# One tile-wide sum of squares and 1/std, an earlier first temporal product, and Gelu's table loaded first, in a four-layer conditional residual kernel

## The chip, the cores and the metric

The kernel runs on one core of a Trainium2 chip, in one launch. The metric is the device time of that launch in microseconds, the median of several runs. "PE" is TensorE, "ACT" ScalarE, "DVE" VectorE, "POOL" GpSimd and "SP" SyncE, which only issues DMAs here.

## What is computed

Four residual layers over x of 4 x 1024 x 512, float32:

```python
x = x + concat(gelu(x @ fc1.T + b1) @ fc2.T + b2, gelu(...) @ expert[idx].T + be)   # 512 -> 2048 -> 384 + 128
x = x + x @ W1[subject].T + b[subject]
ctx   = ema(x, tau_ctx)                                       # over the 1024 time steps
gated = x * sigmoid(concat(x, ctx) @ Wg.T + bg)
mod   = 0.5 + sigmoid(gelu(x @ Wn1.T + bn1) @ Wn2.T + bn2)    # 4 rows
temporal = sum_d softmax(blend)[d] * ema(gated * mod[d], tau[d])
gate  = sigmoid(temporal @ Wtemp.T + btemp)
soma  = gelu(x @ Wsoma.T + bsoma)
o     = (soma * gate) @ Wout.T
x = x + (o - mean) / sqrt(var + 1e-5) * gamma + beta
x = x + x @ W3[idx] + b[idx]
```

## The kernel before, in words

The data lie with the 512 features on partitions, in 4 chunks of 128, and time along the free axis. There are 8 tiles of 512 steps, two for each batch entry. Nearly every matrix product is split: both operands are held as a high part (fp32r) and a low rest, and `split_product` (L971 to L974) issues high x high, high x low and low x high into one PSUM bank. ScalarE makes the high parts (copies), VectorE the low ones (`low_part`, L1261). One output chunk of a 512 x 512 layer is therefore 12 matmuls of 128 x 512, a gate product (`gate`, two inputs) 24.

The order of every engine's work is written out by hand, and engines meet at counting semaphores only. `Once` leaves out a wait that an earlier one implies.

First comes the long part, layers 0 and 1: 128 units (8 tiles x 16 chunks of the hidden layer). PE runs fc1(u) and then fc2(u-2). ScalarE applies Gelu in place (L840), then copies the high part (L844), and VectorE makes the low one. Weights are loaded, split and partly parked in DRAM by the way. In the last tile's units the recurrent layer's first tile begins already: n1(0), mo(0), gate(0,0) to gate(0,3). mod_of(0) (L866) stands at the end of ScalarE's unit 9 of that tile.

Then come the rounds r = 1 to 7, one for each tile. In a steady round PE issues: n1(r), rb(r-2), gate(r,0), mo(r), te(r-1,0..3), gate(r,1), gate(r,2), l3(r-2,0..3), gate(r,3), ou(r-1,0..3), so(r,0), so(r,1), ss(r-1), so_pair(r). Round 1 is joined to the end of the long part and has gate(1,0), l1(7,3), gate(1,1), te(0,..), gate(1,2), gate(1,3), ou(0,..). Here n1 and mo give the modulation (h1_of and mod_of on ScalarE; POOL adds 2, stores the 4 rows and loads them back to all partitions as mod_t). `gate` gives Wg's product. VectorE scans it (scan_g), ScalarE applies tanh, and traces_a to traces_d (VectorE) make the four moving averages of a chunk and their sum `temporal`. `temporal_hi` (ScalarE) and `temporal_low` (VectorE) split it for te. te_tanh, spikes, spikes_hi and spikes_low lead on to ou. `o_of` copies and squares ou's result, and sum_squares adds the four squares into sumsq.

The normalisation before the change: ss multiplies sumsq, four blocks of 128 steps as the weights, by one column of ones (L1146). The sums over the 512 features lie then as 128 x 4. rows_std takes the square root (L811), rows_rstd the reciprocal (L1477), and four tensor_scalar (L1483) write them on the diagonals of `diag`. rb multiplies four of these by ones (L1157), which spreads 1/std over all partitions in PSUM bank 6. z_of multiplies by it and gamma (L1490), x3_of adds beta and the residual (L1496). x3_hi_of and x3_low split the result for l3, whose output y_of reads.

The tail, after round 7, is rb(6), te(7,..), l3(6,0), ou(7,..), l3(6,1), ss(7), l3(6,2), rb(7), l3(6,3), and at last l3(7) chunk by chunk. On VectorE rows_rstd(r-1) stands between traces_c(r,3) and traces_d(r,3), and temporal_low(r) behind them.

Bank 0 serves te(0), ou(0) and the row sums; bank m serves te, ou and l1 of the last tile.

Of the kernel before, what the change touches and what calls it, by code (L numbers as in the profile page):

```python
# [8 lines left out]
ALU = mybir.AluOpType  # L9
# [3 lines left out]
P = 128  # L13
# [28 lines left out]
def build(nc, x, tok16, tok8, small, fc1_w, fc2_w, exp_w, exp_b, l1_w, l1_b, wg, wn1, wsoma, wtemp, wout,  # L42
# [13 lines left out]
    with ctx:  # L56
# [12 lines left out]
        def sem(name):  # L69
# [60 lines left out]
        std = const("std", TOK // P)  # L130
        rstd = const("rstd", TOK // P)
# [3 lines left out]
        diag = const("diag", TOK)  # L135
# [49 lines left out]
                ("L1", "N1", "SO", "MO", "WG", "TE", "OU", "SS", "RB", "L3")}  # L185
# [26 lines left out]
        s_diag = sem("s_diag")  # L212
# [116 lines left out]
        SS_BANK, RB_BANK = bank[0], bank[6]  # L329
# [341 lines left out]
        def _(eng):  # L671
# [135 lines left out]
            def rows_std(i):  # L807
                on.wait_ge(s_pe["SS"], i + 1)
                if i:
                    on.wait_ge(s_rstd, i)  # L810
                eng.activation(std[:, :], SS_BANK[:, 0:TOK // P], ACT.Sqrt, bias=eps_sb[:, 0:1],  # L811
                               scale=1.0 / DIM).then_inc(s_std, 1)
# [16 lines left out]

            fc1_hi(0)  # L830
# [5 lines left out]
            for u in range(UNITS):  # L836
                t, j = divmod(u, HC)
                ps = fc1_bank(u)
                on.wait_ge(s_fc1, u + 1)
# [25 lines left out]
                if t == LAST and j == 9:  # L865
                    mod_of(0)  # L866
# [43 lines left out]
            for m in range(SH):  # L910
                temporal_hi(1, m)

            for r in range(2, NT):
                h1_of(r)
                temporal_hi(r - 1, 3)
# [24 lines left out]
                for m in range(SH):  # L940
                    temporal_hi(r, m)

            temporal_hi(LAST, 3)
# [9 lines left out]
            on.wait_ge(s_rstd, LAST)  # L953
            eng.activation(std[:, 0:1], eps_sb[:, 0:1], ACT.Sqrt).then_inc(s_chain, 1)
# [13 lines left out]
        def _(eng):  # L968
# [75 lines left out]
            def gate(i, m):  # L1044
# [27 lines left out]
                for c in range(KC):  # L1072
                    x2 = slot(i, c)
                    for k, before in ((2 * c, 0), (2 * c + 1, 1)):
# [4 lines left out]
                                           c == KC - 1 and before == 1)  # L1079
                mm.then_inc(s_pe["WG"], 1)  # L1080

            def te(i, m):
                if m == 0:
                    if i:
                        on.wait_ge(s_std, i)
                    else:
                        on.wait_ge(s_x2, KC * NT)
                elif m >= 2:
# [52 lines left out]
            def ss(i):  # L1141
# [3 lines left out]
                for q in range(TOK // P):  # L1145
                    mm = eng.matmul(SS_BANK[:, q:q + 1], sumsq[:, q * P:(q + 1) * P], ones[:, 0:1],  # L1146
                                    start=True, stop=True)
                mm.then_inc(s_pe["SS"], 1)

            def rb(i):  # L1150
                if i < LAST:
                    on.wait_ge(s_gated, KC * (i + 1) + 3)
# [595 lines left out]
```

## Time and profile before

| | us |
|---|---|
| median of 3 runs | 1387.55 (1387.07 to 1387.76) |
| the profiled execution | 1386.63 |
| its span, first to last instruction | 1384.6 |
| PE busy | 1366.0 (99%) |
| DVE busy | 761.2 (55%) |
| ACT busy | 479.9 (35%) |
| POOL busy | 136.2 (10%) |

The span is what the profile covers; the rest of the execution's time lies around it. A row of the time line has its start, its busy time, engine, line, operation, output<-input and count; a bracket tells how long the engine had been idle and whose end released it. Matmuls overlap: one of 128 x 512 is busy for 0.39 us and the next starts 0.23 us after it, so distances are read from start to start. A float32 matmul shows as two records.

### The profile page before, as it was taken

To read this page: it belongs to the slowest core of one execution; us is meant where nothing else is said; L and a number is where in the kernel's file an instruction comes from. 1 tells how busy PE (TensorE), PEld (TensorE's weight loads), DVE (VectorE), ACT (ScalarE), POOL (GpSimd) and SP (SyncE) were. 2 spreads that over 40 slices of the span, in tenths; PEclk is the share of its full clock that TensorE was granted. 3 is DMA by queue.
4 is the path that set the end of the run, shared out by engine and by line. 5 is a ranking of instruction groups with operands and counts; after the bars stand their busy time and mean duration, and the time that the engine had idled before them with its cause. 6 is when DMAs were issued, how large, how long until landed. Compare 5 with 4: busy or idle time off the path is not lost.

```text
span 1384.6 us, 15423 instructions
## 1 busy us (share of the span) xinstructions
PE 1366.0 (99%) x6024; PEld 1119.0 (81%) x6024; DVE 761.2 (55%) x1067; ACT 479.9 (35%) x799; POOL 136.2 (10%) x170
## 2 busy tenths in 40 slices
PE   9999999999999999999999999899999999999998
PEld 7888888888888888888887888678787878787877
DVE  3344242232342332333221793999797979797993
ACT  5443342332342332333221221334334343424253
POOL 5000100000100000000000220013101210032000
PEclk9999999999999999999999999999999999999999
DMA  5423522502532413423133934711232123211201
GB/s 132 137 69 122 137 99 107 152 31 84 154 124 80 129 69 111 127 97 97 41 107 114 219 124 154 177 66 61 92 122 93 61 92 122 92 62 61 92 0 61
DMA packets 68376, 140.91 MB, mean 102 GB/s; under 512 B 7328, under 2 KB 19616, under 8 KB 64336
## 3 DMA queue, kind: packets, MB, share of 16 engines
q1 hardware_dynamic: 61360, 116.71, 26.9%
q0 software_dynamic: 6944, 23.23, 5.6%
q8 instruction: 47, 0.77, 0.2%
q14 instruction: 25, 0.20, 0.1%
HBM read 86.85 MB, written 53.05 MB: 101 GB/s over the span
## 4 chain that ended last, share of the span: by engine, by line
PE 90%; DVE 7%; DMA 1%; issue 1%; ACT 1%; POOL 0%; SPq 0%; DVEq 0%; POOLq 0%; ACTq 0%
PE bank L972 30%; PE bank L973 29%; PE bank L974 29%; DVE drive L1417 2%; DVE drive L1402 1%; DVE temporal L1427 1%; DVE temporal L1417 1%; PE bank L1039 1%; PE bank L1157 0%; DVE spikes_lo L1261 0%; DMA x_slot<-x2hl_dram 0%; DVE bank L1378 0%; DMA mod_t<-mod_dram 0%; PE bank L1146 0%; DMA x_raw<-in_x 0%
## 5 line engine op out<-in xcount | busy, mean ns | idle before, releaser
L1261 DVE TENSOR_TENSOR h_hl<-bank,h_hl 128x512 fp32r<-128x512 f32 x128 | 88.7, 693 | 472.8 <-ACT h_hl L844 472.8
L972 PE MATMUL bank<-x_hl,wa 128*128 128x512 f32 x512 | 199.7, 390 | 1.4 <-DVE h_hl L1261 0.8
L974 PE MATMUL bank<-x_hl,wa 128*128 128x512 f32 x512 | 199.2, 389 | 0.0
L973 PE MATMUL bank<-x_hl,wa 128*128 128x512 f32 x512 | 199.2, 389 | 0.0
L972 PE MATMUL bank<-h_hl,wa 128*128 128x512 f32 x512 | 199.2, 389 | 0.0
L973 PE MATMUL bank<-h_hl,wa 128*128 128x512 f32 x512 | 199.2, 389 | 0.0
L974 PE MATMUL bank<-h_hl,wa 128*128 128x512 f32 x512 | 199.2, 389 | 0.0
L840 ACT ACTIVATE bank<-bank,small_sb 128x512 f32<-128x512 f32 x128 | 84.2, 658 | 216.7 <-PE bank L974 216.5
L844 ACT ACTIVATE h_hl<-bank 128x512 fp32r<-128x512 f32 x128 | 76.7, 599 | 231.5 <-PE bank L974 231.1
L972 PEld LDWEIGHTS bank<-x_hl,wa 128*128 128x128 f32 x512 | 96.1, 188 | 23.7 <-issue 2.7
L974 PEld LDWEIGHTS bank<-x_hl,wa 128*128 128x128 f32 x512 | 96.1, 188 | 20.1
L973 PEld LDWEIGHTS bank<-h_hl,wa 128*128 128x128 f32 x512 | 96.2, 188 | 20.0
L974 PEld LDWEIGHTS bank<-h_hl,wa 128*128 128x128 f32 x512 | 96.1, 188 | 19.9
L972 PEld LDWEIGHTS bank<-h_hl,wa 128*128 128x128 f32 x512 | 96.0, 188 | 19.9
L973 PEld LDWEIGHTS bank<-x_hl,wa 128*128 128x128 f32 x512 | 96.0, 188 | 19.7
L1402 DVE SCALAR_TENSOR_TENSOR drive<-gated,small_sb,mod_t 128x512 f32<-128x512 f32 x128 | 92.1, 740 | 35.9 <-DMA mod_t<-mod_dram 34.2
L972 PE MATMUL bank<-x_slot,wg_hl 128*128 128x512 f32 x256 | 101.2, 395 | 1.3 <-ACT mod_row L740 1.3
L973 PE MATMUL bank<-x_slot,wg_hl 128*128 128x512 f32 x256 | 99.8, 390 | 0.0
L974 PE MATMUL bank<-x_slot,wg_hl 128*128 128x512 f32 x256 | 99.4, 388 | 0.0
L628 POOL DMA_DIRECT2D x2hl_dram<-x_hl x28 | 21.1, 770 | 606.4 <-DVE x_hl L1261 606.4
L1427 DVE TENSOR_TENSOR temporal<-drive,temporal 128x512 f32<-128x512 f32 x96 | 66.1, 688 | 1.2
L1261 DVE TENSOR_TENSOR x_hl<-x_raw,x_hl 128x512 fp32r<-128x512 f32 x96 | 61.7, 685 | 1.3 <-ACT x_hl L718 1.3
(154 smaller groups left out, 2323.8 us busy)
## 6 DMA issues: line engine op xcount, KB each, us to landing
x_slot<-x2hl_dram SPq DMA_DIRECT2D x32, 513.0 KB, 4.8
x2hl_dram<-x_hl POOLq DMA_DIRECT2D x28, 512.0 KB, 9.3
stage<-in_l_w SPq DMA_DIRECT2D x32, 256.0 KB, 3.1
x_dram<-x_raw SPq DMA_DIRECT2D x8, 1024.0 KB, 5.4
xt<-x_dram SPq DMA_DIRECT2D x8, 1024.0 KB, 5.7
mod_t<-mod_dram POOLq DMA_DIRECT2D x8, 1024.0 KB, 4.9
l3w_hl<-l3w_dram SPq DMA_DIRECT2D x16, 512.0 KB, 6.8
x_raw<-in_x SPq DMA_DIRECT2D x7, 1024.0 KB, 9.0
```

The source lines that it names most:

```text
L628: eng.dma_start(x2hl_dram[t, c, :, :, 1:1 + TOK], x_hl[t % 2][:, :, c, :].bitcast(F32)).then_inc(s_hlst[c], 16)
L840: eng.activation(ps[:, :], ps[:, :], ACT.Gelu, bias=fc1_b_sb[:, j:j + 1]).then_inc(s_gelu, 1)
L844: eng.activation(h_hl[u % 2][:, 0, :], ps[:, :], ACT.Copy).then_inc(s_hhi, 1)
L972: eng.matmul(ps, w_hi, x_hi, start=first, stop=False)
L973: eng.matmul(ps, w_hi, x_lo, start=False, stop=False)
L974: return eng.matmul(ps, w_lo, x_hi, start=False, stop=final)
L1039: eng.matmul(mo_bank(i)[0:TAUS, :], wn2_sb, h1[:, :], start=True, stop=True).then_inc(s_pe["MO"], 1)
L1261: return eng.tensor_tensor(lo, raw, hi.bitcast(F32), ALU.subtract)
L1402: eng.scalar_tensor_tensor(drive[d % 2][:, :], gated[:, :], blend_sb[:, TAUS * c + d:TAUS * c + d + 1], mod_t[:, d, :], ALU.mult, ALU.mult ...
L1417: eng.tensor_tensor_scan(traced, alpha[:, 1 + d:2 + d].to_broadcast([P, TOK]), drive[d % 2][:, :], start, ALU.mult, ALU.add).then_inc(s_tr ...
L1427: eng.tensor_tensor(temporal[:, c, :], drive[d % 2][:, :], temporal[:, c, :], ALU.add).then_inc(s_add, 1)
```

## The change

1. A one-column Gelu is ScalarE's first instruction. 2. mod_of(0) moves ahead of the wait for fc1 in its unit. 3. In round 1 gate(1,1) moves behind te(0,..), and VectorE's order there follows (x2_lo and spikes earlier, scan_g(1,1) later); te(0,m) waits for the last tile's x2 chunk by chunk. 4. ss becomes one product of 128 x 128 ones with sumsq, which leaves the sum on every partition; the square root and the reciprocal are taken over 128 x 512 in SBUF, z_of reads that, and diag and rb are gone. 5. mo(r) goes inside gate(r,0), behind its first 6 matmuls, and temporal_hi(r-1,2) behind h1_of(r). 6. rows_rstd(r-1) moves between the two halves of temporal_low(r), in the last round behind both.

```diff
@@ -127,12 +127,10 @@
         eps_sb = const("eps_sb", 1)
         g_last = const("g_last", KC)
         trace_last = const("trace_last", KC * TAUS)
-        std = const("std", TOK // P)
-        rstd = const("rstd", TOK // P)
         zeros = const("zeros", 2)
         ones = const("ones", P)
         ident = const("ident", P)
-        diag = const("diag", TOK)
+        rstd = const("rstd", TOK)
         stage_hi = nc.alloc_sbuf_tensor_at("stage_hi", [P, TOK], F32R, offset=constants_at[0] - 4 * TOK)
 
         bank = [ctx.enter_context(nc.psum_tensor(f"bank{i}", [P, TOK], F32)) for i in range(8)]
@@ -182,7 +180,7 @@
         s_exp = sem("s_exp")
         s_id = sem("s_id")
         s_pe = {k: sem("s_pe_" + k) for k in
-                ("L1", "N1", "SO", "MO", "WG", "TE", "OU", "SS", "RB", "L3")}
+                ("L1", "N1", "SO", "MO", "WG", "TE", "OU", "SS", "L3")}
         s_x2free = sem("s_x2free")
         s_g = sem("s_g")
         s_glast = sem("s_glast")
@@ -209,7 +207,6 @@
         s_ssq = sem("s_ssq")
         s_std = sem("s_std")
         s_rstd = sem("s_rstd")
-        s_diag = sem("s_diag")
         s_z = sem("s_z")
         s_x3 = sem("s_x3")
         s_x3hi = sem("s_x3hi")
@@ -326,7 +323,7 @@
         def l3_bank(i, m):
             return bank[((7, 4, 7, 4) if i < LAST else (1, 2, 3, 5))[m]]
 
-        SS_BANK, RB_BANK = bank[0], bank[6]
+        SS_BANK = bank[0]
 
 
         def x2_at(i, c):
@@ -807,8 +804,11 @@
             def rows_std(i):
                 on.wait_ge(s_pe["SS"], i + 1)
                 if i:
-                    on.wait_ge(s_rstd, i)
-                eng.activation(std[:, :], SS_BANK[:, 0:TOK // P], ACT.Sqrt, bias=eps_sb[:, 0:1],
+                    on.wait_ge(s_z, KC * i)
+                else:
+                    on.wait_ge(s_psthi, 16 * len(PARKED))
+                    on.wait_ge(s_stlo, STAGED)
+                eng.activation(rstd[:, :], SS_BANK[:, :], ACT.Sqrt, bias=eps_sb[:, 0:1],
                                scale=1.0 / DIM).then_inc(s_std, 1)
 
             def x3_hi_of(i, m):
@@ -827,6 +827,9 @@
                 eng.activation(to, l3_bank(i, m)[:, :], ACT.Identity, bias=l3_b_sb[:, b * KC + m:b * KC + m + 1]
                                ).then_inc(s_y, 1)
 
+
+            on.wait_ge(s_cst, 1)
+            eng.activation(g_last[:, 0:1], eps_sb[:, 0:1], ACT.Gelu)
             fc1_hi(0)
             for c in range(KC):
                 x_hi(0, c)
@@ -836,6 +839,8 @@
             for u in range(UNITS):
                 t, j = divmod(u, HC)
                 ps = fc1_bank(u)
+                if t == LAST and j == 9:
+                    mod_of(0)
                 on.wait_ge(s_fc1, u + 1)
                 eng.activation(ps[:, :], ps[:, :], ACT.Gelu, bias=fc1_b_sb[:, j:j + 1]).then_inc(s_gelu, 1)
                 on.wait_ge(s_gelu, u + 1)
@@ -862,8 +867,6 @@
                         l1_hi(b, j - L1_UNIT - KC)
                 if t == LAST and j == 8:
                     h1_of(0)
-                if t == LAST and j == 9:
-                    mod_of(0)
                 if t and x2_unit(t - 1) <= j < x2_unit(t - 1) + 2:
                     x2_hi(t - 1, 2 * (j - x2_unit(t - 1)))
                     x2_hi(t - 1, 2 * (j - x2_unit(t - 1)) + 1)
@@ -907,11 +910,12 @@
             rows_std(0)
             soma_of(1, 2)
             soma_of(1, 3)
-            for m in range(SH):
-                temporal_hi(1, m)
+            temporal_hi(1, 0)
+            temporal_hi(1, 1)
 
             for r in range(2, NT):
                 h1_of(r)
+                temporal_hi(r - 1, 2)
                 temporal_hi(r - 1, 3)
                 mod_of(r)
                 wg_tanh(r, 0)
@@ -937,9 +941,10 @@
                 rows_std(r - 1)
                 soma_of(r, 2)
                 soma_of(r, 3)
-                for m in range(SH):
-                    temporal_hi(r, m)
-
+                temporal_hi(r, 0)
+                temporal_hi(r, 1)
+
+            temporal_hi(LAST, 2)
             temporal_hi(LAST, 3)
             te_tanh(LAST, 0)
             for m in range(KC):
@@ -950,8 +955,8 @@
             for m in range(KC):
                 spikes_hi(LAST, m)
 
-            on.wait_ge(s_rstd, LAST)
-            eng.activation(std[:, 0:1], eps_sb[:, 0:1], ACT.Sqrt).then_inc(s_chain, 1)
+            on.wait_ge(s_z, KC * LAST)
+            eng.activation(rstd[:, 0:1], eps_sb[:, 0:1], ACT.Sqrt).then_inc(s_chain, 1)
             y_of(LAST - 1, 0)
             for m in range(KC):
                 o_of(LAST, m)
@@ -1077,15 +1082,16 @@
                                            x2[:, 0, at:at + TOK],
                                            x2[:, 1, at:at + TOK], c == 0 and not before,
                                            c == KC - 1 and before == 1)
+                    if m == 0 and c == 0 and i > 1:
+                        mo(i)
                 mm.then_inc(s_pe["WG"], 1)
 
             def te(i, m):
-                if m == 0:
-                    if i:
-                        on.wait_ge(s_std, i)
-                    else:
-                        on.wait_ge(s_x2, KC * NT)
-                elif m >= 2:
+                if i == 0:
+                    on.wait_ge(s_x2, KC * LAST + m + 1)
+                elif m == 0:
+                    on.wait_ge(s_std, i)
+                if m >= 2:
                     on.wait_ge(s_soma, KC * i + m + 1)
                 on.wait_ge(s_wtemp, 16 * KC)
                 for c in range(KC):
@@ -1142,21 +1148,8 @@
                 on.wait_ge(s_cst, 1)
                 on.wait_ge(s_sq, KC * i + 1)
                 on.wait_ge(s_ssq, SH * (i + 1))
-                for q in range(TOK // P):
-                    mm = eng.matmul(SS_BANK[:, q:q + 1], sumsq[:, q * P:(q + 1) * P], ones[:, 0:1],
-                                    start=True, stop=True)
-                mm.then_inc(s_pe["SS"], 1)
-
-            def rb(i):
-                if i < LAST:
-                    on.wait_ge(s_gated, KC * (i + 1) + 3)
-                else:
-                    on.wait_ge(s_z, KC * LAST)
-                for q in range(TOK // P):
-                    on.wait_ge(s_diag, (TOK // P) * i + q + 1)
-                    mm = eng.matmul(RB_BANK[:, q * P:(q + 1) * P], ones[:, :], diag[:, q * P:(q + 1) * P],
-                                    start=True, stop=True)
-                mm.then_inc(s_pe["RB"], 1)
+
+                eng.matmul(SS_BANK[:, :], ones[:, :], sumsq[:, :], start=True, stop=True).then_inc(s_pe["SS"], 1)
 
             def l3_part(i, m, c):
                 return split_product(l3_bank(i, m)[:, :], l3w_hl[c][:, 0, m * P:(m + 1) * P],
@@ -1212,17 +1205,13 @@
             mo(1)
             gate(1, 0)
             l1(LAST, 3)
-            gate(1, 1)
             for r in range(1, NT):
                 if r > 1:
                     n1(r)
-                    rb(r - 2)
                     gate(r, 0)
-                    mo(r)
                 for m in range(KC):
                     te(r - 1, m)
-                if r > 1:
-                    gate(r, 1)
+                gate(r, 1)
                 gate(r, 2)
                 if r > 1:
                     for m in range(KC):
@@ -1234,7 +1223,6 @@
                 so(r, 1)
                 ss(r - 1)
                 so_pair(r)
-            rb(LAST - 1)
             for m in range(KC):
                 te(LAST, m)
             l3(LAST - 1, 0)
@@ -1243,7 +1231,6 @@
             l3(LAST - 1, 1)
             ss(LAST)
             l3(LAST - 1, 2)
-            rb(LAST)
             l3(LAST - 1, 3)
             on.wait_ge(s_soma, KC * LAST + 2)
             for c in range(KC):
@@ -1447,11 +1434,10 @@
                 trace_of(i, c, 3)
                 add_of(i, c, 3)
 
-            def temporal_low(i):
-                for p in (0, 2):
-                    on.wait_ge(s_temphi, KC * i + p + 2)
-                    low_part(temporal_lo[:, p:p + 2, :], temporal[:, p:p + 2, :], ts_hi[:, p:p + 2, :]
-                             ).then_inc(s_templo, 2)
+            def temporal_low(i, p):
+                on.wait_ge(s_temphi, KC * i + p + 2)
+                low_part(temporal_lo[:, p:p + 2, :], temporal[:, p:p + 2, :], ts_hi[:, p:p + 2, :]
+                         ).then_inc(s_templo, 2)
 
             def spikes(i, m):
                 on.wait_ge(s_gate, KC * i + m + 1)
@@ -1474,20 +1460,13 @@
 
             def rows_rstd(i):
                 on.wait_ge(s_std, i + 1)
-                eng.reciprocal(rstd[:, :], std[:, :]).then_inc(s_rstd, 1)
+                eng.reciprocal(rstd[:, :], rstd[:, :]).then_inc(s_rstd, 1)
+
+            def z_of(i, m):
                 on.wait_ge(s_rstd, i + 1)
-                on.wait_ge(s_id, 3)
-                if i:
-                    on.wait_ge(s_pe["RB"], i)
-                for q in range(TOK // P):
-                    eng.tensor_scalar(diag[:, q * P:(q + 1) * P], ident[:, :], rstd[:, q:q + 1], None, ALU.mult
-                                      ).then_inc(s_diag, 1)
-
-            def z_of(i, m):
-                on.wait_ge(s_pe["RB"], i + 1)
                 on.wait_ge(s_o, KC * i + m + 1)
                 o = o_of_tile(i)[:, m, :]
-                eng.scalar_tensor_tensor(o, o, gamma_sb[:, m:m + 1], RB_BANK[:, :], ALU.mult, ALU.mult
+                eng.scalar_tensor_tensor(o, o, gamma_sb[:, m:m + 1], rstd[:, :], ALU.mult, ALU.mult
                                          ).then_inc(s_z, 1)
 
             def x3_of(i, m):
@@ -1594,21 +1573,23 @@
             traces_d(0, 3)
             x2_of(LAST, 0)
             x2_of(LAST, 1)
-            temporal_low(0)
+            temporal_low(0, 0)
+            temporal_low(0, 2)
             x2_of(LAST, 2)
             scan_g(1, 0)
             x2_of(LAST, 3)
             traces_a(1, 0)
-            traces_b(1, 0)
             for c in range(KC):
                 x2_lo(LAST, c)
-            scan_g(1, 1)
+            for m in range(SH):
+                spikes(0, m)
+            traces_b(1, 0)
+            spikes(0, 3)
             traces_c(1, 0)
-            traces_d(1, 0)
-            for m in range(KC):
-                spikes(0, m)
             spikes_low(0, 0, 2)
             spikes_low(0, 2, 2)
+            traces_d(1, 0)
+            scan_g(1, 1)
             traces_a(1, 1)
             traces_b(1, 1)
             scan_g(1, 2)
@@ -1622,10 +1603,11 @@
             traces_d(1, 2)
             traces_a(1, 3)
             traces_b(1, 3)
-            rows_rstd(0)
             traces_c(1, 3)
             traces_d(1, 3)
-            temporal_low(1)
+            temporal_low(1, 0)
+            rows_rstd(0)
+            temporal_low(1, 2)
             for r in range(2, NT):
                 norm_of(r - 2)
                 scan_g(r, 0)
@@ -1656,10 +1638,13 @@
                 traces_a(r, 3)
                 traces_b(r, 3)
                 traces_c(r, 3)
-                rows_rstd(r - 1)
                 traces_d(r, 3)
-                temporal_low(r)
-
+                temporal_low(r, 0)
+                if r < LAST:
+                    rows_rstd(r - 1)
+                temporal_low(r, 2)
+
+            rows_rstd(LAST - 1)
             norm_of(LAST - 1)
             spikes(LAST, 0)
             x3_low(LAST - 1, 0, 2)
```

## Rows read from the trace of the kernel before

**Rows 1.** The page: busy us (share of the span), instructions of PE.

```profile
PE 1366.0 (99%) x6024; PEld 1119.0 (81%) x6024; DVE 761.2 (55%) x1067; ACT 479.9 (35%) x799; POOL 136.2 (10%) x170
```

**Rows 2.** Time line of ACT and PE at the start of the kernel.

```profile
3.66 0.63 ACT L676 ACTIVATE wa<-stage_early 128x512 fp32r<-128x512 f32 x1 [1.50 <-DMA stage_early<-in_fc_w]
...
10.19 1.28 ACT L840 ACT_TABLE_LOAD   x1 [0.58 <-PE bank L974]
...
12.44 0.39 PE L974 MATMUL bank<-x_hl,wa 128*128 128x512 f32 x1
13.65 0.47 PE L972 MATMUL bank<-x_hl,wa 128*128 128x512 f32 x1 [0.82 <-DVE h_hl L1261]
```

**Rows 3.** Time line of ACT and PE at mod_of(0) and gate(0,0).

```profile
744.11 0.66 ACT L840 ACTIVATE bank<-bank,small_sb 128x512 f32<-128x512 f32 x1 [5.38 <-PE bank L974]
...
748.10 0.50 PE L972 MATMUL bank<-x_slot,wg_hl 128*128 128x512 f32 x1 [1.31 <-ACT mod_row L740]
```

**Rows 4.** Time line of PE in round 1: ou(0) and ss(0).

```profile
871.38 0.47 PE L972 MATMUL bank<-ts_hi,wout_hl 128*128 128x512 f32 x1 [4.46 <-DVE spikes_lo L1261]
...
891.58 1.04 PE L1146 MATMUL bank<-ones,sumsq 128*128 128x1 f32 x8 [2.00 <-DVE sumsq L1473]
```

**Rows 5.** Time line of PE in the tail.

```profile
1333.97 0.47 PE L972 MATMUL bank<-ts_hi,wtemp_hl 128*128 128x512 f32 x1 [2.52 <-DVE temporal_lo L1261]
...
1348.34 0.47 PE L972 MATMUL bank<-ts_hi,wout_hl 128*128 128x512 f32 x1 [0.52 <-DVE spikes_lo L1261]
...
1362.06 0.95 PE L1146 MATMUL bank<-ones,sumsq 128*128 128x1 f32 x8
1362.87 0.49 PE L972 MATMUL bank<-x_hi,l3w_hl 128*128 128x512 f32 x1
...
1365.73 1.05 PE L1157 MATMUL bank<-diag,ones 128*128 128x128 f32 x8
1366.54 0.48 PE L972 MATMUL bank<-x_hi,l3w_hl 128*128 128x512 f32 x1
...
1369.80 0.50 PE L972 MATMUL bank<-ts_hi,l3w_hl 128*128 128x512 f32 x1 [0.26 <-DVE x_lo L1261]
```

**Rows 6.** Windows: length, busy of PE, PEld, DVE, ACT, POOL; PEclk; DMA.

```profile
871.00:876.00 5.00, 4.62 (x13) 3.70 (x14) 4.96 (x7) 0.31 (x1) 0.00 (x0) 0.66 1.04 152
889.00:896.00 7.00, 5.00 (x20) 3.90 (x19) 6.79 (x9) 3.31 (x5) 0.00 (x0) 0.76 0.00 0
1330.00:1336.00 6.00, 3.39 (x19) 2.71 (x18) 5.97 (x10) 3.14 (x6) 0.00 (x0) 1.00 0.01 3
```

**Rows 7.** Time line of DVE in round 1.

```profile
856.05 1.28 DVE L1417 TENSOR_TENSOR_SCAN temporal<-alpha,trace_last,drive 128x512 f32<-128x512 f32 x1 [13.65 <-PE bank L974]
...
872.28 0.69 DVE L1386 SCALAR_TENSOR_TENSOR gated<-bank,xt 128x512 f32<-128x512 f32 x1
...
907.91 2.35 DVE L1261 TENSOR_TENSOR temporal_lo<-temporal,ts_hi 128x1024 fp32r<-128x1024 f32 x2
```

**Rows 8.** Time line of PE: mo(7) and the start of te(6,0).

```profile
1267.99 1.02 PE L1039 MATMUL bank<-h,small_sb 128*4 128x512 f32 x2
1268.94 0.50 PE L972 MATMUL bank<-ts_hi,wtemp_hl 128*128 128x512 f32 x1
```

**Rows 9.** Groups of DVE by line: busy us, mean ns of one, idle before.

```profile
L1477 DVE RECIPROCAL rstd<-std 128x4 f32<-128x4 f32 x8 | 1.4, 173 | 2.5 <-ACT std L811 2.5
...
L1366 DVE RECIPROCAL alpha<-alpha 128x5 f32<-128x5 f32 x1 | 0.2, 192 | 0.0
...
L1368 DVE TENSOR_SCALAR alpha_minus<-alpha 128x1 f32<-128x1 f32 x1 | 0.2, 154 | 0.0
```

**Rows 10.** Time line of DVE in the last round.

```profile
1321.58 0.68 DVE L1386 SCALAR_TENSOR_TENSOR gated<-bank,xt 128x512 f32<-128x512 f32 x1
...
1329.89 0.88 DVE L1483 TENSOR_SCALAR diag<-ident,rstd 128x128 f32<-128x128 f32 x4
...
1334.88 2.71 DVE L1490 SCALAR_TENSOR_TENSOR o_sb<-o_sb,small_sb,bank 128x512 f32<-128x512 f32 x4
```

## The prediction

> **What bounds the kernel now.** I read the page first: PE is busy for 99% of the span, so a removed TensorE instruction is worth its full spacing wherever the engine does not wait, and the other gains can only be its waits [rows 1]. Then I followed PE in order of time and looked at each bracket (idle time and what ended it). Five places stand out. At the start, the third fc1 unit begins 1.21 us after the product ahead of it, because ScalarE loaded Gelu's table for 1.28 us only once the first unit was there [rows 2]. At 748 us the first gate product waits 1.31 us for mod_of(0) [rows 3]. In round 1 the output product waits 4.46 us for spikes_lo and the sum over rows 2.00 us for sumsq [rows 4]. Before te(LAST) it waits 2.52 us for temporal_lo [rows 5]. Products otherwise follow each other every 0.2275 us (60 of them, 13.72 us less fills, from the start of ou(LAST) to the sum over rows at 1362.06 [rows 5]); so 12, 24 and 48 products are 2.7, 5.45 and 10.9 us.
>
> The clock view shows a second price of the round 1 waits: the granted clock averages 0.66 over 5 us after the first, which is 3.4 us at 1.2 instead of 2.4 GHz, and 0.76 over 7 us around the second, again 3.4 us. Work done at half speed for 3.4 us loses 1.7 us each. Around the 2.52 us wait at 1331 the clock stayed at the upper level [rows 6].
>
> **The change part by part**, in the time of the profiled execution.
>
> (a) Table. The new Gelu of one column waits only for eps_sb and brings the load ahead of the first copy, which anyway starts only at 3.66 us, waiting for a DMA [rows 2]. Then the first real Gelu starts 1.28 us earlier, and fc1(2) would be ready before PE is (13.65 - 1.28 = 12.37, PE at 12.67). PE gets 13.65 - 12.67 = **1.0 us**. The next limit is PE itself.
>
> (b) mod_of(0) ahead of the Gelu: MO's product stands a whole unit ahead of this gate in PE's order, and ScalarE is idle for 5.38 us until 744.11, so the tanh is done before the Gelu and gate(0,0) no longer waits: **1.3 us** [rows 3]. The modulation rows leave earlier on POOL's queue, where nothing is pushed back by it.
>
> (c) te(0) ahead of gate(1,1). PE was ready for ou(0) at 871.38 - 4.46 = 866.9; before that stood te(0) (10.9) and three gate products (16.35), so te(0) can start at 839.6 and ends at 850.5, 5.45 earlier than the 855.97 at which VectorE's trace scan was released. In the 13.65 us VectorE was idle there [rows 7] now fit the four x2_lo and three spikes, seven operations of 0.6 to 0.7 us (4.4 in all). From the scan at 856.05 to gated(1,1) at 872.28 are 16.2 us of work; the 4.4 leave it and a tanh round trip of 0.9 comes in. Gated(1,1) is then at 850.5 + 16.2 - 4.4 + 0.9 = 863.2, nearly **9 us earlier**. spikes_lo is done near 859.5, PE needs it at 866.9: the 4.46 us go, and the low clock after it, 1.7: **6.2 us**. The sum of squares, ready at 891.5, is ready at 882.6; PE, ready at 889.6 before, comes at 889.6 - 6.2 = 883.4. The 2.00 us go too, with their 1.7 of low clock: **3.7 us**, on a margin of only 0.8.
>
> (d) RB. Each broadcast takes 0.81 us from its start to the next product's (1365.73 to 1366.54). Six stand ahead of te(LAST-1): **4.9 us**; the other two are in the tail below. In exchange the sum over rows, 0.81 before (1362.06 to 1362.87), becomes one 512-column float32 product by 128 weights [rows 5]. The nearest row is MO, also float32 with 512 columns: 0.95 from start to start [rows 8]. Bounds: 0.8 (nothing) and 1.4. I take 0.95, 0.15 more, for six **-0.9 us**. MO itself only moves inside gate(r,0). It comes 6 products after n1, at +1.36; the Gelu it needs ends at about 0.16 + 0.1 + 0.69 = 0.95 (the N1 result's end, the start, the activation). So nothing waits, and the modulation starts 4 us earlier.
>
> (e) Reciprocal. VectorE now takes it over 128x512, once a tile, in place of 0.17 and the four diag products (0.88) [rows 9, 10]. No row shows this size. Small ones do: 128x4 takes 173 ns and 128x5 192, while a plain operation on one column takes 154 [rows 9]. That makes 6.3 ns per element (19/3) or 9.5 (38/4), and from the two reciprocals alone 19. If all of it were fixed cost, 512 elements would take about 0.6, as other VectorE operations do. I take 8 ns, between the first two: **R = 4.2 us**. Ends kept for the range: 0.6 and 9.9. The square root goes from 0.26 to 0.66 us as any 128x512 ScalarE operation with a bias [rows 3]; it runs in the table pair that is there now.
> The Trainium skill, in "VectorE: DVE Perf Modes", section "First, the fixed hardware budget", says that Reciprocal is an iterative divide with a repeat count of 8; with that page's 0.96 GHz it is 8.3 ns per element, an estimate of 4.4 us, and the sum would be 0.6 worse than with my value. It speaks against this part of the change.
>
> (f) Where R lands. In most rounds temporal_low(r,0), R, temporal_low(r,2) stand between the last trace and te(r), and PE first runs n1 and the gate. In the last round now the trace chain starts from sumsq: gated at 1321.58, te(LAST) at 1333.97, 12.4 us, less 1.05 for the old reciprocal and diag = 11.35 [rows 5, 10]. With T the start of te(r-1) (1268.94 before [rows 8]), ou ends at T + 49.1 (48 x 4 + 24 products), the last square at 50.5, gated at 51.15, so te's first half is ready at T + 62.5, its second with R at 67.9; PE asks at 70.9 and 72.2. Rounds 3 to 6 have 4 us to spare. **Round 2** has not: the traces of tile 1 end at 907.91 - 8.9 - 1.05 = 897.95 [rows 7], the first low half is ready at 899.3, R follows, the second half at 904.7. PE, from 883.4 on, does 0.95 + 60 products + 0.95 and asks for the first at 898.9, for the second at 900.7. It waits 0.4 + 4.0 = **-4.4 us**, and since this is nearly the wait that took the clock down before [rows 4, 6], **-1.7** more.
>
> (g) Tail. te(LAST) started at T + 65.03, now at T + 62.5. The reciprocal of tile LAST-1 now stands ahead of its norm: z began 0.91 after te's start [rows 5, 10], now 5.1. Four z, four x3 and a spike, nine operations of 0.66, follow, so x3_low begins at 11.0. l3(LAST-1,0), due at 10.9, waits 1.3; the last three spikes come at 13.3 to 15.1, spikes_lo after them, ou at +16.5 instead of 14.37. That is T + 79.0 against 79.4. From ou, the last tile's sum of squares ends at +14.7, square root +15.5, R +19.75, then z, x3, copy and low part (3.0) +22.8, where l3(LAST) began at +21.46 before (1369.80 - 1348.34 [rows 5]). T + 101.8 against 100.86: **-0.9 us**.
>
> **Sum**: 1.0 + 1.3 + 6.2 + 3.7 + 4.9 - 0.9 = 16.2; less 4.4, 1.7 and 0.9 = 9.2 us. The profiled execution took 1386.63 us (span 1384.6), 0.9 under the median 1387.55. 1386.6 - 9.2 = 1377.4, and with the 0.9 near the median 1378.3; I say **1378.0 us**.
>
> **Rivals.**
> - Reciprocal at the speed of other operations (R = 0.6). For it: the operation count is the same as a copy's. Against: it is 19 ns dearer than a plain operation at 128x4. The round 2 wait shrinks to 0.9 and keeps its clock, ou starts at T + 62.5 + 14.4 = 76.9, and l3(LAST) 20.4 later, when PE is free: 97.3, a gain of 3.6. 16.2 - 0.9 + 3.6 = 18.9: 1367.7, against the median 1368.5. Chance 0.15.
> - Slower than before: R is 9.9 us (19 ns per element, the difference of the two reciprocals). Round 2 loses 10.1 + 1.7, the tail 0.9 + 2 x 5.7 = 12.3, and rounds 3 to 6 and the one between are past their slack (62.5 + 9.9 + 1.2 = 73.6 against 72.2), 1.4 five times. 16.2 - 31.1 = -15: about 1402. It decides from R = 4.2 + 9.2/3 = 7.3 us (14 ns per element). For it: only one pair of rows; against: the other two slopes. Chance 0.06, and 0.06 that R lies near 7 and all cancels (1384.8 to 1390.3).
> - The round 1 gain is not had in full: the sum of squares misses its margin of 0.8 us and the clock falls there again, or MO waits for h1 in each of six rounds (0.4 us to spare). Some 3 us dearer: 1381. Chance 0.11.
> - That the table is loaded again: copies and tanhs follow Gelu without a load now, so it would need another set. Its price is (a), 1 us, inside the range.
> My forecast has 0.62. What remains open in it is 1.7 us of clock either way (round 2, or the 2.6 us wait before l3(LAST)).
>
> **Numbers.** About 0.2%, 2.8 us, is what a measurement can tell from no change. Faster 0.88, same 0.06, slower 0.06. The range is 1368 (fast reciprocal, just held) to 1385 (R near 6.5 with both clock losses).
>
> **What would show it.** No PE wait at 13, 748, ou(0) and ss(0), and clock 1.00 there; the sum over rows as two float32 passes with 0.95 to the next product; no broadcast; RECIPROCAL 128x512 near 4.2 us; PE waits 4 us for temporal_lo at te(1) and has a low clock behind it, 1 to 2 us at l3(LAST-1,0) and ou(LAST), 2 to 3 at l3(LAST); none in rounds 3 to 6. The prediction is wrong if the reciprocal is not near 4.2 us, or if te(0)'s move leaves VectorE where it was.

## The result and the profile after

The changed kernel takes **1374.59 us** in the median (4 runs, 1371.03 to 1374.97) beside 1387.65 us of the kernel before on the same chip (4 runs, 1387.07 to 1388.50). The ratio is 0.990, 95% interval 0.9882 to 0.9917: 13.1 us faster. 1378.0 was forecast. Sign and range held, and the gain came out larger. The profiled execution took 1374.9 us (span 1373.2) against 1386.63 before (span 1384.6), 11.7 less where the sum said 9.2.

The page of the changed kernel, engines first, then the group of VectorE's modulation multiplies and the group of its reciprocals (busy us, mean ns, idle time before and what ended it):

```profile
PE 1359.0 (99%) x5912; PEld 1109.7 (81%) x5912; DVE 781.5 (57%) x1035; ACT 480.9 (35%) x799; POOL 134.4 (10%) x170
...
L1389 DVE SCALAR_TENSOR_TENSOR drive<-gated,small_sb,mod_t 128x512 f32<-128x512 f32 x128 | 92.0, 739 | 2.6 <-DMA mod_t<-mod_dram 0.6
...
L1463 DVE RECIPROCAL rstd<-rstd 128x512 f32<-128x512 f32 x8 | 26.8, 3345 | 3.0 <-ACT rstd L811 3.0
```

PE is still busy for 99% [rows 1]. The reciprocal over 512 columns takes 3345 ns, against 173 for the old one [rows 9]. The waits of the changed kernel's PE, grouped (us in total, times, longest):

```profile
PE bank L977 <- DVE temporal_lo L1248: 6.3, 3, 3.2
PE bank L977 <- DVE x_lo L1248: 1.6, 1, 1.6
PE bank L1179 <- DVE eps_sb L1491: 1.2, 1, 1.2
PE bank L977 <- DVE spikes_lo L1248: 0.5, 1, 0.5
```

mod_row and sumsq are gone from that list, and spikes_lo has only the 0.5 of the tail left. temporal_lo, 2.52 in the tail before [rows 5], now has 6.3 in three places. In order of time on the changed kernel's PE (start, us, instruction, idle before):

```profile
746.20 0.39 PE L977 MATMUL bank<-x_slot,wg_hl 128*128 128x512 f32 x1
...
864.74 0.40 PE L977 MATMUL bank<-ts_hi,wout_hl 128*128 128x512 f32 x1
...
881.07 1.02 PE L1152 MATMUL bank<-sumsq,ones 128*128 128x512 f32 x2
...
897.40 0.47 PE L977 MATMUL bank<-ts_hi,wtemp_hl 128*128 128x512 f32 x1 [0.45 <-DVE temporal_lo L1248]
...
898.63 0.39 PE L979 MATMUL bank<-ts_hi,wtemp_hl 128*128 128x512 f32 x1
901.64 0.79 PE L977 MATMUL bank<-ts_hi,wtemp_hl 128*128 128x512 f32 x1 [2.62 <-DVE temporal_lo L1248]
902.24 0.63 PE L978 MATMUL bank<-temporal_lo,wtemp_hl 128*128 128x512 f32 x1
...
914.23 0.39 PE L977 MATMUL bank<-x_slot,wg_hl 128*128 128x512 f32 x1
...
1240.49 1.02 PE L1152 MATMUL bank<-sumsq,ones 128*128 128x512 f32 x2
1240.94 0.80 PE L977 MATMUL bank<-x_slot,wsoma_hl 128*128 128x512 f32 x1
1241.58 0.40 PE L978 MATMUL bank<-x_slot,wsoma_hl 128*128 128x512 f32 x1
...
1256.30 0.40 PE L977 MATMUL bank<-ts_hi,wtemp_hl 128*128 128x512 f32 x1
...
1310.87 1.02 PE L1152 MATMUL bank<-sumsq,ones 128*128 128x512 f32 x2
...
1320.61 0.52 PE L977 MATMUL bank<-ts_hi,wtemp_hl 128*128 128x512 f32 x1 [3.23 <-DVE temporal_lo L1248]
...
1336.58 0.47 PE L977 MATMUL bank<-ts_hi,wout_hl 128*128 128x512 f32 x1 [0.52 <-DVE spikes_lo L1248]
...
1358.45 0.50 PE L977 MATMUL bank<-ts_hi,l3w_hl 128*128 128x512 f32 x1 [1.64 <-DVE x_lo L1248]
```

The rows answer to [rows 3] (746.20), [rows 4] (864.74 and 881.07) and [rows 5] (from 1320.61 on). The first three start without a bracket: the old waits are gone. The new cost stands at te(1). From 897.40 to the next gate product at 914.23 are 16.83 us, where the kernel before needed 11.05, from these rows of its PE:

```profile
910.71 0.50 PE L972 MATMUL bank<-ts_hi,wtemp_hl 128*128 128x512 f32 x1
...
921.76 0.39 PE L972 MATMUL bank<-x_slot,wg_hl 128*128 128x512 f32 x1
```

Of the 5.8 more, 2.8 are the wait (898.63 plus one spacing of 0.23 to 901.64), and 3.0 come from the slow products behind it, whose starts are 0.43 apart instead of 0.23. The windows of the changed kernel show the clock (length, busy of PE, PEld, DVE, ACT, POOL; then PEclk, the granted clock as a share of 2.4 GHz, and DMA):

```profile
866.00:871.00 5.00, 5.00 (x24) 4.14 (x23) 5.00 (x7) 2.38 (x4) 0.00 (x0) 1.00 0.89 304
902.00:908.00 6.00, 6.00 (x15) 4.64 (x15) 6.00 (x9) 0.00 (x0) 0.00 (x0) 0.51 0.43 175
1321.00:1325.00 4.00, 4.00 (x12) 3.14 (x11) 3.96 (x3) 0.00 (x0) 0.00 (x0) 0.59 0.00 0
```

After ou(0) began the clock is at the full 2.4 GHz, where it had been 0.66 [rows 6]. Behind the wait of te(1) it is 1.2 GHz for nearly 6 us, and behind that of te(LAST) again for 3.3 of 4.

Where did the profiled gain come from? The lead of each step's start over the same step before is (gate(r,m) and n1(r) of round r, the others of their tile): gate(0,0) 1.9 us, ou(0) 6.6, ss(0) 10.5, n1(2) 12.2, gate(2,0) 13.9, te(1) 13.3, gate(2,1) 7.5, te(LAST-1) 12.6, te(LAST) 13.4, ou(LAST) 11.8, l3(LAST) 11.35, end 11.4. It climbs through round 1, falls by 5.8 inside te(1), and is won again at a steady 1.0 us a round.

### The profile page after: what moved, and what is told of

It is laid out like the page before. It is cut to its first block, busy times and chain, and to the rows that moved or that the text cites. A ratio compares the mean times of both kernels' runs of the same rounds, so it can differ in the third digit from the quotient of the medians.

```text
span 1373.2 us, 15160 instructions
## 1 busy us (share of the span) xinstructions
PE 1359.0 (99%) x5912; PEld 1109.7 (81%) x5912; DVE 781.5 (57%) x1035; ACT 480.9 (35%) x799; POOL 134.4 (10%) x170
## 4 chain that ended last, share of the span: by engine, by line
PE 93%; DVE 4%; DMA 1%; ACT 1%; issue 0%; SPq 0%; DVEq 0%
PE bank L977 31%; PE bank L978 31%; PE bank L979 31%; DVE drive L1404 1%; DMA x_slot<-x2hl_dram 1%; DVE drive L1389 1%; DVE rstd L1463 0%; PE bank L1044 0%; DVE temporal L1414 0%; PE bank L1152 0%; DMA x_raw<-in_x 0%; DVE temporal L1404 0%; DVE bank L1365 0%; DVE temporal_lo L1248 0%; ACT temporal L827 0%
```

## The experiments

They were timed in three sets (e1 to e4; e5 to e8; e9 and e10). The kernel before took 1390.43, 1389.69 and 1388.77 us in them, so only the ratios compare across sets.

**The changed kernel again** (e8), as the control of the second set.

> The changed kernel itself, on the same chip as the others of this set, to compare them with it. All theories: 12 to 15 us below the kernel before. By my theory of the low clock its runs spread over 3 to 4 us, one or two losses of 1.7 us or more after the waits in te(1) and before te(7) being there or not, while those waits themselves (2.6 and 3.2 us) stay.

Measured: 1375.76 us, ratio 0.9896 (0.9879 to 0.9912), -13.9 us. The two long waits are the same, 2.62 at te(1) and 3.23 at te(LAST). The four runs spread over 4.0 us, as expected. Between its first weight and 60 us PE waits 4.5 us in all, where the first trace has 0.4. The longest is 1.82; the Gelu ahead of it stood behind a weight copy of ScalarE that had itself waited 2.98 us for its load:

```profile
43.34 0.47 PE L977 MATMUL bank<-x_hl,wa 128*128 128x512 f32 x1 [1.82 <-DVE h_hl L1248]
```

**The normalisation alone** (e1): parts (d) to (g), with te(0), the gate order, mod_of(0) and the table as before. (MO stays where it was too.)

```diff
-                for q in range(TOK // P):
-                    mm = eng.matmul(SS_BANK[:, q:q + 1], sumsq[:, q * P:(q + 1) * P], ones[:, 0:1],
+                eng.matmul(SS_BANK[:, :], ones[:, :], sumsq[:, :], start=True, stop=True)
...
-            rb(LAST - 1)
...
+                eng.reciprocal(rstd[:, :], rstd[:, :]).then_inc(s_rstd, 1)
```

> The changed normalisation alone on the kernel before: no early table, mod_of(0), te(0), VectorE's round 1 and mo(r) where they were. My theory: the broadcast's products are worth 1.0 us a round (five rounds 5.1) and 1.6 in round 2, but the reciprocal of 3.35 us between the two halves of temporal_low then makes PE wait about 2.2 us in te(1), with 1.7 to 3 us of low clock behind it, and the tail gives 1 us back: 1 to 4.5 us faster than before, that is 1383 to 1386.5. The waits of 4.5 us before ou(0) and 2.0 before ss(0) stay. Rival: the normalisation carries most of the gain, as its 8 broadcasts and 8 sums are the only TensorE work that changes: 8 us or more faster.

Measured: 1384.42 us, ratio 0.9961 (0.9948 to 0.9975), **-6.0 us**, more than the 1 to 4.5 that I expected. The profiled execution doesn't show as much: its span ends 2.9 us under the first trace of the kernel before (1381.7 against 1384.6), after 0.47 lost at the start. The old waits at ou(0) (4.46) and ss(0) (2.29, where it had been 2.00) stay, and te(LAST) waits 3.24. te(1) waits only 1.95, with the clock at 1.00 behind it. The reason lies one step earlier, and e2 below shows it: behind ss(0) the clock is low here, so that PE comes to te(1) later after ss(0).

**te(0)'s move alone** (e10): part (c) on the kernel before, old normalisation.

```diff
             l1(LAST, 3)
-            gate(1, 1)
...
-                if r > 1:
-                    gate(r, 1)
+                gate(r, 1)
```

(and with it VectorE's order of round 1, and te(0,m) waiting for x2 chunk by chunk.)

> The kernel before with te(0) ahead of gate(1,1) and VectorE's new order of round 1, nothing else: diag, RB and the reciprocal over 128x4 stay. My theory: the waits before ou(0) and ss(0) and the low clock behind them go (10 us), RB of tile 0 waits about 1 us longer for diag, and te(1) has no wait, since that one is the long reciprocal's: 9 us faster than before. Rival: VectorE is short in round 2 without the reciprocal as well: te(1) waits 2 us or more and the gain is 4 to 6.

Measured: 1379.59 us, ratio 0.9937 (0.9923 to 0.9951), **-9.2 us**. Its PE in time order:

```profile
866.71 0.40 PE L972 MATMUL bank<-ts_hi,wout_hl 128*128 128x512 f32 x1
...
883.04 0.95 PE L1145 MATMUL bank<-ones,sumsq 128*128 128x1 f32 x8
...
894.29 1.13 PE L1156 MATMUL bank<-diag,ones 128*128 128x128 f32 x8 [1.86 <-DVE diag L1480]
```

Both waits and both stretches of low clock are gone. te(1) has no wait either: that one belongs to the long reciprocal. The broadcast instead waits 1.86 for diag, which the full change doesn't have, since it has no broadcast.

**te(0)'s move undone** (e2), all else as changed: the same lines in the other direction.

> The changed kernel with te(0) behind gate(1,1) again, and VectorE's order of round 1 with it. My theory: this move is worth 8.6 us (4.5 + 2.0 of waits and 1.6 to 1.7 of low clock after each, less fills) and the wait in te(1) stays about as long, since VectorE and PE are later by the same: 1383. Rival: most of it is only moved to te(1), so that without it te(1) has no wait: the wait of 2.8 us and 3.1 of low clock there go, and the time is 1377 to 1378.

Measured: 1385.18 us, ratio 0.9962 (0.9949 to 0.9976), -5.25 us, so some 9 us (0.9962 against the control's 0.9896) are lost without the move. The waits at ou(0) (4.46) and ss(0) (1.57) are back, and te(1) keeps its 0.45 and 2.62, as expected:

```profile
906.59 0.47 PE L977 MATMUL bank<-ts_hi,wtemp_hl 128*128 128x512 f32 x1 [0.45 <-DVE temporal_lo L1250]
...
910.84 0.50 PE L977 MATMUL bank<-ts_hi,wtemp_hl 128*128 128x512 f32 x1 [2.62 <-DVE temporal_lo L1250]
```

The windows behind ss(0), of e1 and then of this run:

```profile
892.00:900.00 8.00, 7.96 (x26) 5.81 (x27) 7.93 (x10) 5.58 (x7) 0.00 (x0) 0.80 0.29 87
```

```profile
890.00:898.00 8.00, 8.00 (x34) 6.26 (x35) 7.93 (x10) 6.96 (x10) 0.00 (x0) 1.00 0.42 133
```

Both runs lack the move, and VectorE takes 17.75 us from the start of the sum of squares to te(1)'s first low half in both (889.62 to 907.37, 887.48 to 905.23), as in the changed kernel (878.28 to 896.03). PE takes 17.32 us from ss(0) to te(1) in e1 without a wait, and 16.70 here with one of 0.45. So the shorter wait of e1 goes with the low clock (and the longer sum product, 2.05 us) ahead of it, not with the missing move.

**Parts (a) and (b) undone** (e9).

```diff
-            on.wait_ge(s_cst, 1)
-            eng.activation(g_last[:, 0:1], eps_sb[:, 0:1], ACT.Gelu)
...
-                if t == LAST and j == 9:
-                    mod_of(0)
```

(mod_of(0) stands behind the unit's Gelu again.)

> The changed kernel without the early Gelu and with mod_of(0) behind the Gelu of its unit again. My theory: both gains are PE's waits and nothing later makes them up: 0.8 us before the third fc1 unit and 1.3 us at gate(0,0) are back, with their fills 2.4 us, 1377 to 1378 where the changed kernel is at 1375. Rival: the first weights' arrival paces the start, so the table's part is lost in it: only 1.5 us slower.

Measured: 1376.24 us, ratio 0.9909 (0.9895 to 0.9922). The control's ratio was 0.9896, so 1.8 us with overlapping intervals: the timing alone doesn't show it, and it can't tell my 2.4 from the rival's 1.5. In the trace the waits of 0.79 (h_hl, third unit) and 1.31 (mod_row, gate(0,0)) are there, which the changed kernel doesn't have. Whether the first of them is worth its microsecond is another question. Eight traces have the early Gelu (the first, e2 to e8). Seven of them show PE waits of 0.2 to 1.8 us somewhere between 18 and 56 us, and none of the four without it does (before, e1, e9, e10). gate(0,0) starts at 746.2 to 750.0 with it, 747.7 in the mean, and at 748.0 to 748.6 without it, 748.3 in the mean, of which about 1.4 is mod_row's wait and its slow start. Up to that wait the kernels with the early Gelu are thus 0.8 us later in the mean, not 1.0 earlier: (b)'s gain is seen there, (a)'s is not, and the rival stands, that the loads pace the start. Why the later waits come is open; the sets ran on different chips.

**MO back behind the gate** (e7).

```diff
-                    if m == 0 and c == 0 and i > 1:
-                        mo(i)
...
                     gate(r, 0)
+                    mo(r)
```

> The changed kernel with mo(r) behind gate(r,0) again and temporal_hi(r-1,2) ahead of h1_of(r). My theory: VectorE waits some 5 us more for mod_t in each round, but the chain starts anew from ou's squares, so te(2) to te(7) do not notice: within 0.5 us of the changed kernel, and te(1) has the same waits. Rival: the earlier modulation is what keeps VectorE ahead of PE, so that without it te(r) waits in every round: 5 us or more slower than the changed kernel.

Measured: 1375.57 us, 0.2 from the control in the same set. VectorE's wait for mod_t is 18.6 us with MO back, 34.2 in the kernel before and 0.6 with the change. None of it can be seen at PE: 18 us of idle time taken off an engine, worth nothing that can be measured.

**The reciprocal behind both halves of temporal_low** (e3). My theory was that the wait in te(1) is the reciprocal's place in VectorE's order.

```diff
             temporal_low(1, 0)
-            rows_rstd(0)
             temporal_low(1, 2)
+            rows_rstd(0)
```

(and in each later round but the last, where it stood there already.)

> The changed kernel with the reciprocal behind both halves of temporal_low in every round. My theory: the wait of 2.6 us in the midst of te(1,0) is the reciprocal's alone, and the low clock of 6 us behind it (3.1 us lost) is the wait's: both go, 5.9 us faster than the changed kernel, 1368.7. Rival: the low clock comes whatever the wait (the 0.45 us before te(1) is enough): only 2.8 us faster, 1371.8.

Measured: 1370.85 us, ratio 0.9864 (0.9849 to 0.9879), **-19.6 us**. The ratio lies 4.4 to 5.0 us under the changed kernel's (0.9896 and 0.9900), less than the 5.9 expected and more than the rival's 2.8. The waits in te(1) are gone, and the clock there is 1.00. A smaller one takes their place in l3(0,2): l3(0) now needs 12.2 us (919.52 to 931.68) for 10.9 to 11.0, since ScalarE's y for this bank stands behind a gate's copy and tanh, which waited 4.1 us for VectorE's scan. te(LAST) still waits 3.23, ou(LAST) 1.06 instead of 0.52. From the trace of this version, VectorE, then PE:

```profile
896.20 2.35 DVE L1248 TENSOR_TENSOR temporal_lo<-temporal,ts_hi 128x1024 fp32r<-128x1024 f32 x2
898.47 3.35 DVE L1463 RECIPROCAL rstd<-rstd 128x512 f32<-128x512 f32 x1
```

```profile
928.82 0.50 PE L977 MATMUL bank<-x_hi,l3w_hl 128*128 128x512 f32 x1 [0.97 <-ACT y_sb L827]
```

**temporal_hi(LAST) ahead of the last two somas** (e4). The trace of the changed kernel shows why te(LAST) waits longer than worked out. ScalarE, then VectorE:

```profile
1316.74 1.37 ACT L777 ACTIVATE soma<-bank,small_sb 128x512 f32<-128x512 f32 x2 [1.68 <-PE bank L979]
1318.00 2.17 ACT L756 ACTIVATE ts_hi<-temporal 128x512 fp32r<-128x512 f32 x4
```

```profile
1319.24 2.36 DVE L1248 TENSOR_TENSOR temporal_lo<-temporal,ts_hi 128x1024 fp32r<-128x1024 f32 x2 [1.65 <-ACT ts_hi L756]
```

The copies stand behind two Gelus that wait for PE. The edit, for the last tile alone:

```diff
                 rows_std(r - 1)
+                if r == LAST:
+                    for m in range(KC):
+                        temporal_hi(LAST, m)
                 soma_of(r, 2)
                 soma_of(r, 3)
```

(and out of their old places.)

> The changed kernel with ScalarE's four temporal_hi of the last tile ahead of its soma_of(7,2) and (7,3). My theory: te(7) waits 3.2 us for ScalarE, which takes the two Gelus first, not for VectorE's traces: te(7) starts 1.7 us earlier and all behind it, and with the shorter wait the low clock behind it (1.6 us) may go too: 1371.3 to 1372.9. Rival: VectorE's traces are the limit, as in my prediction: no change, 1374.6.

Measured: 1372.90 us, ratio 0.9878 (0.9863 to 0.9894), -17.5 us, some 2.5 to 3 under the changed kernel by the ratios. te(1) keeps its 2.62 and its low clock. VectorE and PE now:

```profile
1317.49 2.35 DVE L1250 TENSOR_TENSOR temporal_lo<-temporal,ts_hi 128x1024 fp32r<-128x1024 f32 x2
```

```profile
1318.85 0.47 PE L979 MATMUL bank<-ts_hi,wtemp_hl 128*128 128x512 f32 x1 [1.50 <-DVE temporal_lo L1250]
```

The low parts follow the traces without a gap, and the wait is 1.50. From ss(LAST-1) to te(LAST) are 8.0 us instead of 9.74. 0.4 and 0.6 of it come back as waits at l3(LAST-1,0) and ou(LAST).

**Both orders together** (e5).

> The reciprocal behind both halves of temporal_low, and the last tile's temporal_hi ahead of two Gelus, together. My theory: the two are 420 us apart and add up: 2.8 us for te(1) and 1.7 for te(7), against the changed kernel, less 0.9 lost at l3(0,2) and 1 in the tail's norm, plus the low clock that went after both waits (1.7 to 3 us each, where it is there): 3 to 7 us faster than the changed kernel. Rival: the tail's norm (waits before l3(6,0), ou(7) and l3(7)) takes all of the second gain: no faster than the reciprocal's move alone, 3 to 4 us.

Measured: **1369.98 us** (1369.38 to 1370.29), ratio 0.9856 (0.9840 to 0.9873), 5.8 us under the control. It beats both kernels. The clock windows of this version, at te(1) and te(LAST):

```profile
900.00:908.00 8.00, 8.00 (x36) 6.35 (x35) 7.96 (x8) 0.45 (x1) 3.43 (x3) 1.00 0.20 81
1316.00:1324.00 8.00, 7.62 (x34) 6.32 (x35) 7.96 (x9) 2.99 (x4) 0.00 (x0) 1.00 0.00 0
```

**A shorter reciprocal** (e6): it covers 128 of the 512 time steps, and 1/std of the other 384 is left out.

```diff
-                eng.reciprocal(rstd[:, :], rstd[:, :]).then_inc(s_rstd, 1)
+                eng.reciprocal(rstd[:, 0:P], rstd[:, 0:P]).then_inc(s_rstd, 1)
```

> The changed kernel with the reciprocal over 128 of the 512 steps only (384 steps of 1/std are left out, so this part of the output is scaled wrongly): some 0.9 us for 3.35. My theory, that the reciprocal costs about three times its length (once in te(1), twice in the tail, less what other waits hide): the wait of 2.6 us in te(1) falls to 0.2 and its low clock goes, the wait of 1.6 before l3(7) goes, the one before ou(7) and the 3.2 before te(7) stay: 4 to 7 us faster than the changed kernel. Rival: the reciprocal is hidden nearly everywhere and the waits have other causes: under 1.5 us.

Measured: 1369.37 us, ratio 0.9859 (0.9842 to 0.9875), 6.4 under the control. The second wait in te(1) is down to 0.23 at full clock and the one at l3(LAST) is gone; the first in te(1) (0.40) and te(LAST)'s 3.23 stay.

So the reciprocal's length costs the changed kernel about 6 us. The orders of e3 and e4 together give 5.8 without shortening it, but not all of it in the same places: in e5 the 1.64 before l3(LAST) stays, and 1.7 come from te(LAST), where the reciprocal had no part.

## Why the prediction was right, and where its sizes were off

- **(a) Table**: the wait is gone, and in the first trace its time is gained: a few products into the third unit 0.9 for 1.0 (the first product began 0.46 later in this execution, so the net lead stood at 0.43). Over all traces the gain is not shown. The working ended with "the next limit is PE itself", and in seven of the eight traces with the early Gelu PE waits again before 60 us (e9).
- **(b) mod_of(0)**: right. gate(0,0) adds 1.5 for 1.3. The wait is 1.30 or 1.31 in the four kernels that lack this part and absent in the others.
- **(c) te(0)**: right in mechanism and size. Gated(1,1) is at 861.40 (863.2 forecast), both waits and both low clocks are gone, 10.3 us from gate(0,0) to n1(2) for 9.9. The rival of an incomplete gain fell, and e10 shows 9.2 by itself.
- **(d) Broadcast and sum over rows**: this is the term that was mis-sized. Six broadcasts at 0.81 less six sums at 0.15 were 4.0 us; the traces give 6.8. The first part is a wait that I had not listed, 0.52 for diag at the broadcast of round 2 (below), which with its slow start makes 1.7 of gate(2,0)'s lead. The rest is five later rounds at 1.0 instead of 0.66. The distance to the first product behind the broadcast, 0.81 [rows 5], is not all: the second starts 1.13 us behind the broadcast's start, which is 0.90 more than a plain spacing. And the sum over rows is not 0.15 dearer. From its start to the second product behind it are 1.09 us (1240.49 to 1241.58), against 1.13 for the four small products (1323.68 to 1324.81) and 1.30 for MO (1267.99 to 1269.29). MO was the wrong neighbour. A round without a wait, from sum to sum, is 71.47 us before (1252.21 to 1323.68) and 70.38 after (1240.49 to 1310.87): 1.09, of which some 0.14 are in neither term; what they are stays open.

PE of the kernel before, at the broadcast of round 2 and at two sums over rows:

```profile
903.19 1.13 PE L1157 MATMUL bank<-diag,ones 128*128 128x128 f32 x8 [0.52 <-DVE diag L1483]
...
1252.21 0.94 PE L1146 MATMUL bank<-ones,sumsq 128*128 128x1 f32 x8
...
1323.68 0.95 PE L1146 MATMUL bank<-ones,sumsq 128*128 128x1 f32 x8
```

- **(e) Reciprocal**: 3.35 us for 4.2, 6.5 ns per element. That is near the lowest of my three slopes, from the plain operation to the reciprocal of four columns (19/3 = 6.3), and not the value of 8 that I took; from 128x4 to 128x512 it is 6.2 (3172 ns over 508 columns). By the Trainium skill, "VectorE: DVE Perf Modes", section "First, the fixed hardware budget", I had an estimate of 4.4, and this case's measurement is a quarter below it. The rivals of 0.6 and 9.9 fell.
- **(f) Round 2**: right place, and a right sum by luck, from two wrong parts. Waits 0.45 and 2.62 for 0.4 and 4.0 (the shorter reciprocal and the earlier second half), but the clock stayed low for some 6 us, not 3.4: 3.0 lost for 1.7. That is 6.2 in all for 6.1. In four other executions the clock was low for 3.3 us only, and in one it stayed high (last section). Rounds 3 to 6 have no wait on it. e3 and e6 show that the reciprocal's place and length set it.
- **(g) Tail**: -0.9 forecast, -1.3 measured. With T the start of te(LAST-1), the chain to te(LAST) was worked out on VectorE alone: T + 62.5. It came at T + 64.3 (1320.61 - 1256.30), since ScalarE takes two somas ahead of the copies. e4, with that order changed, brings te(LAST) forward by 1.74, to T + 62.6. Its 1.6 us of low clock were not forecast. The later steps made up for most of that, ou at te + 15.97 (16.5) and l3(LAST) at ou + 21.87 (22.8), because the reciprocal is shorter. The wait of 1.3 forecast at l3(LAST-1,0) did not come, since the slow products of te(LAST) hid it; at full clock it is 0.43 (e4).
- **The sum**: 9.2 forecast against 11.4 at the end of the span. (d) makes up 2.8 of the difference, the rest cancels to -0.6. From profile to median another 1.4 come in: the profiled execution of before lay 1.0 below its median, that of after 0.3 above.
- **MO**: nothing, and e7 finds nothing.

So the forecast named what happens and where. Its closeness, 1378.0 for 1374.59, is in part luck: in (f) two errors cancel, and only because the profiled execution had the longest low clock at te(1) of all.

Do the parts add up? The move alone brings 9.2, and everything without the move 5.25 (e2): 14.4, near the 13.1 and 13.9 measured together. The normalisation alone brought 6.0, and with it, the move and (a) and (b) the count would be some 17. The excess thus lies between e1 and e2, which both lack the move. In the traces e1 waits less in te(1) (1.95 at full clock; e2 has 0.45 and 2.62 with 0.79 over 8 us), after losing time to a low clock behind ss(0) that e2 doesn't have. What the clock did in each execution differs, so the 6.0 can't be split further.

## What to carry to other kernels

When work is taken off one engine and given to another as one long operation, its length matters less than what stands behind it in that engine's order: here 3.35 us in front of half an operand made te(1) 3 to 6 us longer, by what the clock did behind the wait, and behind it l3(0) 1.2 us longer. Work out the time of a step that joins two engines on both queues, since a copy behind someone else's wait is late by that wait. And measure a small group of instructions by the distance between plain products on either side of it, not to the first start behind it.

## What the runs showed that was not expected

- **The same wait, another clock.** A wait of 2.62 to 2.64 us in te(1) was followed by a granted clock of 0.79 to 0.81 over 8 us in e2, e4, e8 and e9 (1.2 GHz for some 3.3 us), by nearly 6 us of 1.2 GHz in the changed kernel's first trace, and by none in e7 (1.00), whose kernel differs in MO's place. The wait of 3.2 us before te(LAST) gave 0.63 over 8 us in e8, 0.65 in e7, 0.82 in e6 and 1.00 in e3. What decides stays open: no run varied it on purpose. It may be part of the spread: the changed kernel's four runs in e8's set lie between 1374.3 and 1378.3, those of e5 in the same set, whose clock is 1.0 in all four, within 0.9 us. The windows behind the wait in e8 and in e7:

```profile
905.47:913.47 8.00, 8.00 (x28) 6.52 (x29) 7.07 (x10) 1.56 (x4) 0.23 (x1) 0.79 0.36 131
```

```profile
902.78:910.78 8.00, 8.00 (x35) 6.61 (x36) 7.07 (x10) 1.56 (x4) 0.34 (x1) 1.00 0.39 131
```

- **The float32 sum with 512 columns costs no more than four with one column.** 1.09 against 1.13 us to the second product behind, while MO, with 4 columns of weights, costs 1.30.
- **The start differs by execution.** From the first weight to 60 us PE's waits were 0.4 us in all in one trace of the changed kernel and 4.5 in the other. Such differences sit in every comparison of two single traces, and they are larger than the gain of (a).
